# Layer norm of a cross-attention block: centering on ScalarE by the mean alone, rstd and gamma in one DVE operation in slot 3

## The chip, the cores and the metric
One core of one Trainium2 chip runs the whole program. The metric is device time in microseconds. The kernel before took 670.51 us (median of 3 runs, 669.41 to 670.66).

## The reference
A cross-attention block over 8 batches: 224 queries and 750 keys of width 512, 16 heads of 32.
```
q = queries @ Wq.T + bq;  k = keys @ Wk.T + bk;  v = values @ Wv.T + bv      (keys = values = ctx)
att = softmax(q k^T / sqrt(32));  out = concat_heads(att v) @ Wo.T + bo + queries
mean, var over the last axis (512)
out = (out - mean) / sqrt(var + 1e-5) * gamma + beta
```
The change touches only the last line. All inputs and outputs are float32.

## The kernel before, in words
Batches follow each other in one software pipeline. An iteration has 32 steps, in 4 slots of 8 (`UNIT`); one step does the scores of half a head (112 queries against 750 keys). A slot is one unit of 4 heads. In the steps, PE also does tasks for other batches: it transposes context and x, projects K, Q and V of the next batch, and in steps 18 and 21 (`O_STEPS`) projects the two halves (q = 0, 1) of the output of the batch before. The iterations are b = 0 to 7 and a last one, b = 8 (`B`), without scores, which only drains the pipeline: the tail. In b = 7 (`LAST`) there is no next batch, so from step 12 on PE has only scores, exponent scores, attention and the two output projections to do.

Each engine runs its own list in the order in which the code writes it; the waits are semaphores. The order of one step:
- PE: scores of the next step (`scores`, L523), for which the row maximum of two steps before must have been read from its bank (`RING` = 2); scores with keys on partitions for the exponential (L547); attention times v (`attend`, L563) and the column sums (`sum_keys`, L589); the task of the step (L512, L475).
- ScalarE: the high part of a saved task (L672, L674), the copy of the attention (L698), the maxima (`save_maxima`, L679, first step of a slot), the exponentials (`exp`, L690), the high part of the attention (`attn_high`, L704).
- DVE: the row maximum (`row_max`, L793), the save of a task (`save_task`, L755 to L770), reciprocals (L800), the attention scaling (L807) and its low part (L817), and at the end of a step the layer norm.
- GpSimd: the sums over keys of each head, three additions (L902, L907, L910) in steps 4, 5, 7 and the first step of the next slot, and its part of the layer norm.
- SP starts all DMAs, also in order: after the loads of the next inputs it stores half 0 (`store_half`, L383), fills the stacks of unit 0 of the next batch (`fill_stack`, L377 to L380, 16 DMAs), stores half 1, fills unit 1, and loads the residual (L368).

The layer norm of the batch before runs in this order. Step 19 or 22: DVE writes y = projection + residual from PSUM (L767) and its statistics (L770). Step 20 or 23: mean and variance (`mean_of`, L773). Same step, GpSimd: rstd (`rstd_of`, L920 and L922, a power of -0.5). Step 21 or 24: DVE's `center` (L777) subtracts the mean and multiplies by rstd. Steps 24 to 27: GpSimd multiplies by gamma (L926) and adds beta (L930), half 0 in steps 24 and 25, half 1 in steps 26 and 27. Then the half is stored. In the tail `center` comes in steps 22 and 25; GpSimd does gamma and beta of half 0, and DVE those of half 1 (L783, L785).

Of the kernel before, what the change touches and what calls it, by code (L numbers as in the profile page):

```python
# [7 lines left out]
ALU = mybir.AluOpType  # L8
ACT = mybir.ActivationFunctionType
# [6 lines left out]
def build(nc, x, ctx_tokens, Wq, bq, Wk, bk, Wv, bv, Wo, bo, gamma, beta, out):  # L16
# [68 lines left out]

    LN_STEP = 3 * UNIT
    SUM_STEPS = ((1, 4, 0), (1, 5, 1), (1, 7, 2), (2, 0, 3))
# [83 lines left out]
    with ExitStack() as stack:  # L171
# [71 lines left out]
        recip_ready, attn_scaled, attn_low_saved = sem("recip_ready"), sem("attn_scaled"), sem("attn_low_saved")  # L243
        last_sums_ready, last_scaled, last_ready = sem("last_sums_ready"), sem("last_scaled"), sem("last_ready")
        stats_ready, mean_ready, centered, bias_ready = sem("stats_ready"), sem("mean_ready"), sem("centered"), sem("bias_ready")
# [3 lines left out]
        pair_sums_ready, two_sums_ready, head_sums_ready = sem("pair_sums_ready"), sem("two_sums_ready"), sem("head_sums_ready")  # L249
        const_ready, resid_ready, var_eps_ready, rstd_ready = sem("const_ready"), sem("resid_ready"), sem("var_eps_ready"), sem("rstd_ready")  # L250
        y_scaled, y_ready = sem("y_scaled"), sem("y_ready")

# [104 lines left out]
        def _(sp):  # L357
# [55 lines left out]
            def iteration(b, parity):  # L413
# [13 lines left out]
                def store_half(q):  # L427
                    if q == 1 and isinstance(b, int) and b == B:
                        sp.wait_ge(last_ready, 1)
                    else:  # L430
                        sp.wait_ge(y_ready, 2 * (b - 1) + q + 1)
                    store(b - 1, q)
# [231 lines left out]
        def _(act):  # L664
# [28 lines left out]
            def copy_attn(u):  # L693
# [4 lines left out]
                nc.scalar.copy(attn_sums[:], source[:, :, 0:NQ]).then_inc(attn_copied, 1)  # L698

            def attn_high(u, g, task_n):  # L700
                act.wait_ge(attn_scaled, u + 1)
                if task_n is not None:
                    act.wait_ge(task_ready, task_n)
                nc.scalar.activation(attn_parts[:, 0, g, :], attn[:], ACT.Identity,  # L704
                                     bias=bias16["v"][:, g:g + 1]).then_inc(attn_high_saved, 1)
# [6 lines left out]
            def iteration(b, parity):  # L712
                tasks = iteration_tasks(b)
                before = tasks_before(b)
                for s in range(STEPS):
# [13 lines left out]
                    for u, g_u in due("high", b, s):  # L729

                        after_o = before + tasks[O_STEPS[1]][1] + 1 if g_u == 0 and has_output(b) else None
                        attn_high(u, g_u, after_o)
                    u = unit_before(b, g, 1)
                    if u is not None:
# [9 lines left out]
        def _(dve):  # L744
# [29 lines left out]

            def center(q, batch):
                dve.wait_ge(rstd_ready, 2 * batch + q + 1)
                nc.vector.tensor_scalar(y[0:QP, q], y[0:QP, q], mean_var[0:QP, q, 0:1], rstd[0:QP, q:q + 1],  # L777
                                        ALU.subtract, ALU.mult).then_inc(centered, 1)

            def gamma_beta(q, batch):  # L780

                dve.wait_ge(centered, 2 * batch + q + 1)
                nc.vector.tensor_tensor(y[0:QP, q], y[0:QP, q], rows["gamma"][0:QP], ALU.mult).then_inc(last_scaled, 1)  # L783
                dve.wait_ge(last_scaled, 1)
                nc.vector.tensor_tensor(y[0:QP, q], y[0:QP, q], rows["beta"][0:QP], ALU.add).then_inc(last_ready, 1)  # L785
# [48 lines left out]
            def iteration(b, parity):  # L834
                tasks = iteration_tasks(b)
                before = tasks_before(b)
                for s in range(STEPS):
# [24 lines left out]
                    for u, g_u in due("low", b, s):  # L862
                        attn_low(u, g_u)
                    last = isinstance(b, int) and b == B
                    wait_for_rstd = 4 if last else 3
                    if has_output(b) and s - wait_for_rstd in O_STEPS:
                        center(O_STEPS.index(s - wait_for_rstd), b - 1)
                        if last and s - wait_for_rstd == O_STEPS[1]:
                            dve.wait_ge(rows_loaded, 3 * DMA)
                            gamma_beta(1, b - 1)  # L870

# [6 lines left out]
        def _(pool):  # L878
# [44 lines left out]

            def times_gamma(q, batch):
                pool.wait_ge(centered, 2 * batch + q + 1)
                nc.gpsimd.tensor_tensor(y[0:QP, q], y[0:QP, q], rows["gamma"][0:QP], ALU.mult).then_inc(y_scaled, 1)  # L926

            def plus_beta(q, batch):
                pool.wait_ge(y_scaled, 2 * batch + q + 1)
                nc.gpsimd.tensor_tensor(y[0:QP, q], y[0:QP, q], rows["beta"][0:QP], ALU.add).then_inc(y_ready, 1)  # L930

            pool.wait_ge(rows_loaded, 3 * DMA)

            def iteration(b, parity):
                for s in range(STEPS):
# [5 lines left out]
                    if has_output(b):  # L941
                        for q in range(2):
                            if s == 9 + q:
                                add_bo(q, b - 1)
                            if s == O_STEPS[q] + 2:
                                rstd_of(q, b - 1)
                        last = isinstance(b, int) and b == B
                        for q in range(1 if last else 2):
                            at = O_STEPS[1] + 3 if last else LN_STEP + 2 * q
                            if s == at:  # L950
                                times_gamma(q, b - 1)
                            if s == at + 1:
                                plus_beta(q, b - 1)
# [24 lines left out]
```

## Time and profile before
The profiled execution took 670.35 us, with a span of 668.5 us from its first to its last instruction.

| | busy us | share of the span | instructions |
|---|---|---|---|
| PE (TensorE matmul) | 644.6 | 96% | 5441 |
| DVE (VectorE) | 480.5 | 72% | 680 |
| ACT (ScalarE) | 334.2 | 50% | 657 |
| POOL (GpSimd) | 456.0 | 68% | 458 |

The mean granted clock of PE is 0.988 of full speed. The chain of waits that ended last is 76% PE, 12% GpSimd, 5% DVE, 2% ScalarE. Matmuls are pipelined and their ends modelled, so a busy PE may hold small waits; a share is a mean over stages with different limits. The stretches, timelines and chains below give the time from the start of the span.

### The profile page before, as it was taken

To read this page: it belongs to the slowest core of one execution; us is meant where nothing else is said; L and a number is where in the kernel's file an instruction comes from. 1 tells how busy PE (TensorE), PEld (TensorE's weight loads), DVE (VectorE), ACT (ScalarE), POOL (GpSimd) and SP (SyncE) were. 2 spreads that over 40 slices of the span, in tenths; PEclk is the share of its full clock that TensorE was granted. 3 is DMA by queue.
4 is the path that set the end of the run, shared out by engine and by line. 5 is a ranking of instruction groups with operands and counts; after the bars stand their busy time and mean duration, and the time that the engine had idled before them with its cause. 6 is when DMAs were issued, how large, how long until landed. Compare 5 with 4: busy or idle time off the path is not lost.

```text
span 668.5 us, 15116 instructions
## 1 busy us (share of the span) xinstructions
PE 644.6 (96%) x5441; PEld 450.0 (67%) x5441; DVE 480.5 (72%) x680; ACT 334.2 (50%) x657; POOL 456.0 (68%) x458
## 2 busy tenths in 40 slices
PE   9999999999999999999999999999999999999893
PEld 8766676766777666776767667776677667665452
DVE  4676667778777686776767787776877777677775
ACT  4423645555455455554455554554555544555460
POOL 9302765876957688576858769576885868678942
PEclk9999999999999999999999999999999999999888
DMA  9383322231232223332133312322233201331010
GB/s 289 120 219 87 91 67 72 60 90 50 76 99 70 66 74 83 88 73 86 52 82 90 91 50 76 100 66 70 74 85 90 63 2 28 83 90 39 15 43 28
DMA packets 39562, 53.08 MB, mean 79 GB/s; under 512 B 13436, under 2 KB 25736, under 8 KB 39496
## 3 DMA queue, kind: packets, MB, share of 16 engines
q1 hardware_dynamic: 39496, 52.16, 29.2%
q8 instruction: 46, 0.75, 0.5%
q14 instruction: 20, 0.16, 0.1%
HBM read 24.52 MB, written 3.67 MB: 42 GB/s over the span
## 4 chain that ended last, share of the span: by engine, by line
PE 76%; POOL 12%; DVE 5%; issue 4%; ACT 2%; POOLq 0%; ACTq 0%; DVEq 0%
PE ps_task L512 34%; PE ps_scores L523 9%; PE ps_task L563 9%; PE ps_scoresT L547 8%; POOL pair_sums L902 6%; PE ps_task L475 6%; POOL head_sums L907 3%; POOL head_sums L910 2%; PE ps_scores L512 2%; PE ps_task L589 2%; ACT probsT L690 2%; DVE top L793 2%; PE ps_task L485 1%; DVE y L767 1%; DVE parts L755 1%
## 5 line engine op out<-in xcount | busy, mean ns | idle before, releaser
L793 DVE TENSOR_REDUCE top<-ps_scores 112x1 f32<-112x750 f32 x256 | 235.8, 928 | 115.6 <-PE ps_scores L523 114.5
L902 POOL TENSOR_TENSOR pair_sums<-probsT 125x672 f32<-125x672 f32 x122 | 199.1, 1632 | 163.5 <-ACT probsT L690 160.1
L690 ACT ACTIVATE probsT<-ps_scoresT 125x448 f32<-125x448 f32 x384 | 193.0, 545 | 156.8 <-PE ps_scoresT L547 153.9
L523 PE MATMUL ps_scores<-stacks 96*112 96x512 f16 (+1 forms) x512 | 126.6, 329 | 5.3 <-DVE top L793 4.1
L512 PE MATMUL ps_task<-wvT,ctxT 128*125 128x512 f16 x564 | 129.9, 380 | 0.8 <-DVE ctxT L757 0.7
L512 PE MATMUL ps_task<-ctxT,wkT 128*128 128x375 f16 x708 | 122.7, 323 | 0.1
L547 PE MATMUL ps_scoresT<-stacks 100*125 100x224 f16 x768 | 120.9, 264 | 2.0 <-ACT probsT L690 0.2
L547 PEld LDWEIGHTS ps_scoresT<-stacks 100*125 100x125 f16 x768 | 87.8, 138 | 35.0 <-ACT probsT L690 10.8
L512 PEld LDWEIGHTS ps_task<-wvT,ctxT 128*125 128x125 f16 x564 | 74.6, 136 | 40.0 <-DVE ctxT L757 0.9
L512 PEld LDWEIGHTS ps_task<-ctxT,wkT 128*128 128x128 f16 x708 | 68.7, 97 | 37.5 <-DVE v L760 0.5
L907 POOL TENSOR_TENSOR head_sums<-pair_sums 125x224 f32<-125x224 f32 x122 | 85.2, 698 | 10.4
L910 POOL TENSOR_TENSOR head_sums<-head_sums,pair_sums 125x224 f32<-125x224 f32 x122 | 80.9, 663 | 9.6
L563 PE MATMUL ps_task<-probsT,v 125*32 125x224 f32 x1488 | 81.3, 360 | 0.4 <-ACT attn_sums L698 0.4
L523 PEld LDWEIGHTS ps_scores<-stacks 96*112 96x112 f16 x512 | 59.2, 131 | 29.5 <-issue 18.3
L760 DVE COPY v<-ps_task 125x512 f32<-125x512 f32 x47 | 32.5, 692 | 43.1 <-PE ps_task L512 43.1
L563 PEld LDWEIGHTS ps_task<-probsT,v 125*32 125x32 f32 x1488 | 44.0, 110 | 27.9 <-issue 9.0
L672 ACT ACTIVATE parts<-ps_task,bk 128x375 f16<-128x375 f32 x59 | 33.8, 574 | 49.8 <-PE ps_task L512 49.8
L800 DVE RECIPROCAL recip<-attn_sums 128x112 f32<-128x112 f32 x64 | 53.5, 840 | 3.2 <-ACT attn_sums L698 3.2
L698 ACT COPY attn_sums<-ps_task 128x448 f32<-128x448 f32 x31 | 16.5, 533 | 71.7 <-PE ps_task L589 71.3
L475 PE MATMUL ps_task<-woT,attn_parts 128*112 128x512 f16 x192 | 44.3, 381 | 0.3
L512 PE MATMUL ps_task<-xT,wqT 128*128 128x224 f16 x360 | 39.4, 259 | 0.0
L755 DVE SCALAR_TENSOR_TENSOR parts<-ps_task,bk,parts 128x375 f16<-128x375 f32 x59 | 35.2, 597 | 1.0 <-ACT parts L672 1.0
(94 smaller groups left out, 592.0 us busy)
## 6 DMA issues: line engine op xcount, KB each, us to landing
stacks<-parts SPq DMA_DIRECT2D x256, 60.9 KB, 2.0
ctx_in<-in_ctx SPq DMA_DIRECT2D x16, 672.0 KB
stacks<-parts SPq DMA_DIRECT2D x128, 46.9 KB, 2.0
x_in<-in_x SPq DMA_DIRECT2D x8, 448.0 KB, 3.7
resid<-in_x SPq DMA_DIRECT2D x8, 448.0 KB, 3.8
out_y<-y SPq DMA_DIRECT2D x16, 224.0 KB, 2.3
stacks<-parts SPq DMA_DIRECT2D x128, 14.0 KB, 1.8
ctx_in<-in_ctx SPq DMA_DIRECT2D x16, 78.0 KB
```

Of the source, the lines that this page charges most:

```text
L475: last = nc.tensor.matmul(bank[0:QP, :], attn_parts[:, a, k, QP * q:QP * q + QP], wT["o"][:, c, k, :], start=(k == 0 and (a, c) == (0, 0)) ...
L512: last = nc.tensor.matmul(dst, lhsT, rhs, start=first, stop=(n_mm == 0))
L523: last = nc.tensor.matmul(ps_scores[0:QP, s % RING, keys], stacks[0:STACK_ROWS, g, h, NK + QP * q:NK + QP * q + QP], stacks[0:STACK_ROWS, ...
L547: last = nc.tensor.matmul(ps_scoresT[0:KP, piece % 2, NQ * i:NQ * i + NQ], stacks[:, g, h, KP * k:KP * k + KP], stacks[:, g, h, Qc], start ...
L563: last = nc.tensor.matmul(ps_attn[c:c + DK, 0:NQ], v[of_batch][0:KP, k, P * g + c:P * g + c + DK], probsT[0:KP, g % 2, h, k, :], start=(k ...
L690: nc.scalar.activation(probsT[0:KP, g % 2, h, 2 * j:2 * j + 2, :].rearrange("p k q -> p (k q)"), ps_scoresT[0:KP, piece % 2, 0:2 * NQ], AC ...
L755: nc.vector.scalar_tensor_tensor(dst, src, b16, high, ALU.add, ALU.subtract).then_inc(task_saved, 1)
L793: nc.vector.tensor_reduce(top[0:QP, g % 2, HG * q + h:HG * q + h + 1], ps_scores[0:QP, s % RING, 0:NK], AX.X, ALU.max).then_inc(top_ready, 1)
L800: nc.vector.reciprocal(recip[:, cols], attn_sums[:, 1, cols]).then_inc(recip_ready, 1)
L902: nc.gpsimd.tensor_tensor(pair_sums[0:KP], probsT[0:KP, g % 2, h, 0:3, :], probsT[0:KP, g % 2, h, 3:6, :], ALU.add).then_inc(pair_sums_rea ...
L907: nc.gpsimd.tensor_tensor(head_sums[0:KP, g % 2, h, :], pair_sums[0:KP, 0], pair_sums[0:KP, 1], ALU.add).then_inc(two_sums_ready, 1)
L910: nc.gpsimd.tensor_tensor(head_sums[0:KP, g % 2, h, :], head_sums[0:KP, g % 2, h, :], pair_sums[0:KP, 2], ALU.add).then_inc(head_sums_read ...
```

## The change
ScalarE gets `center`: y becomes mean - y, with the mean as bias column and a scale of -1, in steps 21 and 24, in the tail as well. GpSimd turns gamma's sign once, ahead of the first iteration, so that the product with it has the right sign. DVE's `times_gamma` multiplies y by rstd and by the turned gamma in one operation, in steps 26 and 28 (`GAMMA_STEPS`). GpSimd adds beta in steps 27 and 29. In the tail DVE adds beta to both halves, right behind each product, and GpSimd none. `store_half` waits in the tail for `last_ready` of its half.
```diff
@@ -83,7 +83,7 @@
             NU - 1: {"copy": 11, ("invert", 0): 12, ("invert", 1): 13, "scale": 14, "high": 15, "low": 16}}
     HIGH_STEP, LOW_STEP = STAGES["high"][1], STAGES["low"][1]
 
-    LN_STEP = 3 * UNIT
+    GAMMA_STEPS = (3 * UNIT + 2, 3 * UNIT + 4)
     SUM_STEPS = ((1, 4, 0), (1, 5, 1), (1, 7, 2), (2, 0, 3))
     assert UNIT + LOW_STEP < O_STEPS[0] and O_STEPS[1] < 2 * UNIT + HIGH_STEP
     STEP_OF = {t: s for s, t in {**OWN, **NEXT, **OUTPUT}.items()}
@@ -241,13 +241,14 @@
         top_ready, task_saved = sem("top_ready"), sem("task_saved")
         top_zero = sem("top_zero")
         recip_ready, attn_scaled, attn_low_saved = sem("recip_ready"), sem("attn_scaled"), sem("attn_low_saved")
-        last_sums_ready, last_scaled, last_ready = sem("last_sums_ready"), sem("last_scaled"), sem("last_ready")
+        last_sums_ready, last_ready = sem("last_sums_ready"), sem("last_ready")
         stats_ready, mean_ready, centered, bias_ready = sem("stats_ready"), sem("mean_ready"), sem("centered"), sem("bias_ready")
 
         ones_ready, ident_zero, ident_ready = sem("ones_ready"), sem("ident_zero"), sem("ident_ready")
         pick_zero, pick_ready = sem("pick_zero"), sem("pick_ready")
         pair_sums_ready, two_sums_ready, head_sums_ready = sem("pair_sums_ready"), sem("two_sums_ready"), sem("head_sums_ready")
         const_ready, resid_ready, var_eps_ready, rstd_ready = sem("const_ready"), sem("resid_ready"), sem("var_eps_ready"), sem("rstd_ready")
+        gamma_turned = sem("gamma_turned")
         y_scaled, y_ready = sem("y_scaled"), sem("y_ready")
 
         def need(eng, s, value):
@@ -425,8 +426,8 @@
                     load_ctx(b + 2, half)
 
                 def store_half(q):
-                    if q == 1 and isinstance(b, int) and b == B:
-                        sp.wait_ge(last_ready, 1)
+                    if isinstance(b, int) and b == B:
+                        sp.wait_ge(last_ready, q + 1)
                     else:
                         sp.wait_ge(y_ready, 2 * (b - 1) + q + 1)
                     store(b - 1, q)
@@ -697,6 +698,12 @@
                 source = (ps_attn if not is_last(u) else ps_scores[:, 0]).rearrange("p (a q) -> p a q", a=2)
                 nc.scalar.copy(attn_sums[:], source[:, :, 0:NQ]).then_inc(attn_copied, 1)
 
+            def center(q, batch):
+
+                act.wait_ge(mean_ready, 2 * batch + q + 1)
+                nc.scalar.activation(y[0:QP, q], y[0:QP, q], ACT.Identity, bias=mean_var[0:QP, q, 0:1],
+                                     scale=-1.0).then_inc(centered, 1)
+
             def attn_high(u, g, task_n):
                 act.wait_ge(attn_scaled, u + 1)
                 if task_n is not None:
@@ -730,6 +737,8 @@
 
                         after_o = before + tasks[O_STEPS[1]][1] + 1 if g_u == 0 and has_output(b) else None
                         attn_high(u, g_u, after_o)
+                    if has_output(b) and s - 3 in O_STEPS:
+                        center(O_STEPS.index(s - 3), b - 1)
                     u = unit_before(b, g, 1)
                     if u is not None:
                         for piece in pieces_of(b, s, True):
@@ -772,16 +781,15 @@
             def mean_of(q):
                 nc.vector.bn_aggr(mean_var[0:QP, q], stats[0:QP, q]).then_inc(mean_ready, 1)
 
-            def center(q, batch):
+            def times_gamma(q, batch):
+
+                dve.wait_ge(centered, 2 * batch + q + 1)
                 dve.wait_ge(rstd_ready, 2 * batch + q + 1)
-                nc.vector.tensor_scalar(y[0:QP, q], y[0:QP, q], mean_var[0:QP, q, 0:1], rstd[0:QP, q:q + 1],
-                                        ALU.subtract, ALU.mult).then_inc(centered, 1)
-
-            def gamma_beta(q, batch):
-
-                dve.wait_ge(centered, 2 * batch + q + 1)
-                nc.vector.tensor_tensor(y[0:QP, q], y[0:QP, q], rows["gamma"][0:QP], ALU.mult).then_inc(last_scaled, 1)
-                dve.wait_ge(last_scaled, 1)
+                nc.vector.scalar_tensor_tensor(y[0:QP, q], y[0:QP, q], rstd[0:QP, q:q + 1], rows["gamma"][0:QP],
+                                               ALU.mult, ALU.mult).then_inc(y_scaled, 1)
+
+            def last_beta(q, batch):
+                dve.wait_ge(y_scaled, 2 * batch + q + 1)
                 nc.vector.tensor_tensor(y[0:QP, q], y[0:QP, q], rows["beta"][0:QP], ALU.add).then_inc(last_ready, 1)
 
             def row_max(s, T, unit):
@@ -861,13 +869,11 @@
                         scale_attn(u)
                     for u, g_u in due("low", b, s):
                         attn_low(u, g_u)
-                    last = isinstance(b, int) and b == B
-                    wait_for_rstd = 4 if last else 3
-                    if has_output(b) and s - wait_for_rstd in O_STEPS:
-                        center(O_STEPS.index(s - wait_for_rstd), b - 1)
-                        if last and s - wait_for_rstd == O_STEPS[1]:
-                            dve.wait_ge(rows_loaded, 3 * DMA)
-                            gamma_beta(1, b - 1)
+                    if has_output(b) and s in GAMMA_STEPS:
+                        dve.wait_ge(gamma_turned, 1)
+                        times_gamma(GAMMA_STEPS.index(s), b - 1)
+                        if isinstance(b, int) and b == B:
+                            last_beta(GAMMA_STEPS.index(s), b - 1)
 
             batches(dve, iteration)
 
@@ -921,15 +927,12 @@
                 pool.wait_ge(var_eps_ready, 2 * batch + q + 1)
                 nc.gpsimd.tensor_tensor(rstd[0:QP, q:q + 1], var_eps[0:QP, q:q + 1], minus_half[0:QP], ALU.pow).then_inc(rstd_ready, 1)
 
-            def times_gamma(q, batch):
-                pool.wait_ge(centered, 2 * batch + q + 1)
-                nc.gpsimd.tensor_tensor(y[0:QP, q], y[0:QP, q], rows["gamma"][0:QP], ALU.mult).then_inc(y_scaled, 1)
-
             def plus_beta(q, batch):
                 pool.wait_ge(y_scaled, 2 * batch + q + 1)
                 nc.gpsimd.tensor_tensor(y[0:QP, q], y[0:QP, q], rows["beta"][0:QP], ALU.add).then_inc(y_ready, 1)
 
             pool.wait_ge(rows_loaded, 3 * DMA)
+            nc.gpsimd.tensor_scalar(rows["gamma"][0:QP], rows["gamma"][0:QP], -1.0, None, ALU.mult).then_inc(gamma_turned, 1)
 
             def iteration(b, parity):
                 for s in range(STEPS):
@@ -944,12 +947,8 @@
                                 add_bo(q, b - 1)
                             if s == O_STEPS[q] + 2:
                                 rstd_of(q, b - 1)
-                        last = isinstance(b, int) and b == B
-                        for q in range(1 if last else 2):
-                            at = O_STEPS[1] + 3 if last else LN_STEP + 2 * q
-                            if s == at:
-                                times_gamma(q, b - 1)
-                            if s == at + 1:
+                        for q in range(2):
+                            if s == GAMMA_STEPS[q] + 1 and not (isinstance(b, int) and b == B):
                                 plus_beta(q, b - 1)
 
             batches(pool, iteration)
```

## Rows read from the trace of the kernel before

**Rows 1.** Busy time in stretches of 1 us: stretch, length, busy of each engine, PEclk, DMA.
```profile
609.00:610.00 1.00, 0.38 (x3) 0.26 (x3) 1.00 (x2) 0.26 (x1) 1.00 (x1) 1.00 0.51 125
...
628.00:629.00 1.00, 0.05 (x1) 0.09 (x2) 1.00 (x2) 0.00 (x0) 0.92 (x2) 0.81 0.00 0
629.00:630.00 1.00, 1.00 (x5) 0.79 (x6) 1.00 (x2) 0.00 (x0) 1.00 (x2) 0.50 0.07 16
...
638.00:639.00 1.00, 1.00 (x10) 0.30 (x7) 0.99 (x2) 0.55 (x2) 1.00 (x1) 0.57 0.77 211
```

**Rows 2.** Chain that ended last, 624 to 642 us: start, us, what.
```profile
626.13 1.82 DVE y L777
627.95 0.86 DVE top L793
...
628.95 0.84 PE ps_scores L523 x2
...
638.81 0.57 PE ps_scoresT L547 x4
```

**Rows 3.** Timeline of PE, last batch: start, us, what, idle before and its releaser.
```profile
614.97 0.53 PE L523 MATMUL ps_scores<-stacks 96*112 96x512 f16 x2
...
616.33 0.53 PE L523 MATMUL ps_scores<-stacks 96*112 96x512 f16 x2
...
625.89 0.59 PE L563 MATMUL ps_task<-probsT,v 125*32 125x224 f32 x8
...
640.21 0.41 PE L532 MATMUL ps_scoresT<-ident,top 112*128 112x112 f32 x2
```

**Rows 4.** Timeline of GpSimd, last batch.
```profile
626.06 1.60 POOL L902 TENSOR_TENSOR pair_sums<-probsT 125x672 f32<-125x672 f32 x1
```

**Rows 5.** Groups of instructions: what, times (x), busy us, mean ns of one, idle before.
```profile
L704 ACT ACTIVATE attn_parts<-attn,bv 128x224 f16<-128x224 f32 x32 | 15.4, 482 | 2.6 <-DVE attn L807 2.6
...
L783 DVE TENSOR_TENSOR y<-y,gamma_row 112x512 f32<-112x512 f32 x1 | 1.6, 1564 | 0.1
...
L785 DVE TENSOR_TENSOR y<-y,beta_row 112x512 f32<-112x512 f32 x1 | 0.7, 692 | 0.0
```

**Rows 6.** Lines L777 and L817 alone: duration ns min/median/max.
```profile
L777 DVE TENSOR_SCALAR y<-y,mean_var,rstd x16: 531/1243/1825, 160.6 to 662.0; 112x512 f32<-112x512 f32 x16
...
L817 DVE SCALAR_TENSOR_TENSOR attn_parts<-attn,bv,attn_parts x32: 420/443/1773, 88.4 to 656.1; 128x224 f16<-128x224 f32 x32
```

**Rows 7.** Chain that ended last, the tail.
```profile
659.02 0.18 DVE mean_var L773
...
660.50 0.45 DVE y L777
...
661.97 1.49 DVE y L777
...
665.15 0.69 DVE y L785
```

**Rows 8.** Loop: the stretch 240 to 260; timelines of DVE, PE, GpSimd and SP's queue.
```profile
240.00:260.00 20.00, 20.00 (x179) 14.55 (x177) 15.40 (x24) 10.45 (x21) 17.83 (x19) 1.00 0.20 57
...
257.18 0.44 DVE L755 SCALAR_TENSOR_TENSOR parts<-ps_task,bq,parts 128x224 f16<-128x224 f32 x1
...
259.14 2.08 PE L512 MATMUL ps_task<-ctxT,wkT 128*128 128x375 f16 x12
...
256.31 1.61 POOL L902 TENSOR_TENSOR pair_sums<-probsT 125x672 f32<-125x672 f32 x1
...
252.49 0.51 SPq L379 DMA_DIRECT2D stacks<-parts  x1
```

**Rows 9.** Timeline of DVE, last batch.
```profile
624.09 0.91 DVE L793 TENSOR_REDUCE top<-ps_scores 112x1 f32<-112x750 f32 x1
...
628.72 0.84 DVE L800 RECIPROCAL recip<-attn_sums 128x112 f32<-128x112 f32 x1
...
638.15 5.03 DVE L812 TENSOR_REDUCE head_sums<-probsT 125x224 f32<-125x1344 f32 x2
```

## The prediction

> **What bounds the kernel now.** I read four views in this order: the busy time in stretches, the timelines of the last batch, the chain of waits that ended last, and the groups of instructions with their durations.
>
> The stretches first. In the body of the run TensorE (PE) has no free moment: 20.00 of 20.00 us between 240 and 260 us, at full clock [rows 8]. An engine other than PE can therefore bring nothing there by being quicker; it can only do harm by being late. The reader is to see in the one-microsecond stretches that this ends in the last batch: PE is all but idle in 628 to 629 (0.05 busy), its granted clock drops there (mean 0.81), stands at 0.50 (the 1.2 GHz level) in 629 to 630 and is back in 638 to 639 (0.57) [rows 1]. The chain of waits names what held PE: the centering of half 1 on DVE (L777) starts at 626.13 after GpSimd's rstd, takes 1.82, then the row maximum behind it takes 0.86, then PE's scores start at 628.95 [rows 2]. PE's last matmuls before that end at 626.48 [rows 3], so the hole is 2.47 us. PE then does four steps (one pair of score matmuls each) from 628.95 to 638.81, 2.46 each [rows 2], where the same step took 1.36 at full clock (614.97 to 616.33) [rows 3].
>
> The tail is a second place that ends the run: after PE's last matmul the chain is DVE and GpSimd alone, with the centering of half 1 at 661.97 (1.49), gamma on DVE (1.57) and beta (0.69), ending at 665.84; 2.66 of the span of 668.5 follow, the last store [rows 7].
>
> **Part 1: the slots before the last one (steps 21 and 24 of each batch).** Two L777 go from DVE and two ScalarE instructions of 112x512 come. No row shows such a one. The nearest is L704, SBUF to SBUF with a bias column, 0.482 for 224 columns [rows 5]: below, 0.48; above, 1.10 if it all scaled with the columns. I take 0.7, nearer the low end, because time doesn't scale with the columns in the rows of DVE either (0.69 for 512 [rows 5], 0.44 for 224 [rows 6]). In the last batch it stands behind the two exponentials of step 21 and behind the copy of the maxima in step 24, while PE runs the output projection or has two steps without exponentials; both ends fit in these holes, so it costs nothing. If that cover were gone it would delay the exponentials behind it by its own 0.7. It needs the mean alone, so ScalarE does not wait for GpSimd's rstd. Gain in the loop: none, since PE was never idle for these (above).
>
> **Part 2: slot 3 (steps 26 and 28).** DVE gets two operations with two SBUF inputs of 512 columns. The nearest row is the addition of beta, L785, 0.69 [rows 5]; below 0.53 (the shortest L777 [rows 6]); above, what another engine adds: the same shape took 1.56 (L783) while GpSimd was in an operation of its own [rows 5], and the longest L777 is 1.82 against 0.53 at least [rows 6]. In the last batch L777 from 626.13 ended at 627.95, 0.29 after GpSimd's operation that began at 626.06 and took 1.60 [rows 2, 4]: DVE waited until it had ended. So one operation costs 0.69, and up to 1.3 more if it meets the long pair sum of GpSimd.
>
> The SBUF page of the Trainium skill (SBUF — State Buffer, the part with the port rules) says that a DVE instruction with two SBUF inputs and a GpSimd instruction that reads SBUF lock each other out, whichever comes second waiting for all of the first. That speaks against putting the new operation at step 28, beside GpSimd's sums. The 0.29 and the 1.56 above agree. By the rule step 28 pays the wait in every batch and the sum is the one below; without it the loop term would be zero and the last batch 0.9 better.
>
> In the loop, step 28: the operation comes at 256.35, GpSimd is by then in the pair sum of the second head (at 256.31 before [rows 8], at some 255.7 now, with two operations fewer ahead of it), so I give it 1.5. The row maximum and the save of the Q task move back: that save stands at 257.18 before, ending at 257.6, and PE takes the bank at 259.14 [rows 8]. 1.5 later it ends at 259.1, so PE waits 0 to 0.1: 6 full batches, 0 to 0.6 in sum, I take +0.2. Step 26 meets an idle GpSimd (gamma is no longer there) and a DVE with a pause; nothing waits.
>
> **Part 3: GpSimd.** It loses 15 multiplications, keeps 14 of the betas, now behind the sums of step 29, and gains one multiplication by -1 at the start, when it has nothing else to do before the first head sums. The first store is issued when beta of half 0 is done, some 1.7 later than before in the loop. SP has the 16 stack transfers of the next batch behind it, but those wait for the Q save of about the same moment (issued from 252.49 [rows 8]). The scores that need the first head come behind PE's task of 259.14 [rows 8]: over 6.5 us for four transfers issued 0.6 apart. The second store stood behind these transfers anyway. Cost 0; without this cover it would be the delay itself, 0.3 a batch.
>
> **Part 4: the last batch.** Walk DVE from the end of the row maximum at 625.0 [rows 9]. Up to the last row maximum stand 6 of them (0.87 apart, back to back), 2 reciprocals (0.84 [rows 9], 0.8 apart), two new operations at 0.69, and two attention operations of 0.44 (the median of L817 [rows 6]): 5.2 + 1.6 + 1.4 + 0.9 = 9.1, so 634.1 if nothing blocks. Four of these read two SBUF tensors while GpSimd is busy almost without a gap; each may wait up to 1.3, in all 5.2: 639.3. Walking both engines side by side, GpSimd ends its operation 0.3 to 0.5 into two of them: I take 0.9 in all, 635.0. PE alone could be there at 626.48 + 4 x 1.36 + 1.4 = 633.3. It needs that last row maximum for the transposes at 640.21 [rows 3]. So these begin at 635.1: **-5.1**, made of 2.5 of stall and 4.4 of clock less 1.8 of new, shorter waits of PE for row maxima. Ends: -6.9 (PE alone) and -0.9 (blocked every time). GpSimd has two multiplications less before its next head sums; DVE's own two head sums (5.03 from 638.15 [rows 9]) shift by 3.1, end near 640.1, and the matmuls that take them come at about 641.5, so they hold nothing. Everything behind moves by the same amount.
>
> Will the clock stay? The new waits are 0.4 to 0.8 each, 1.8 in some 8 us. At 609 to 610 PE was busy 0.38 of 1.00, with smaller holes in the three microseconds before, and the clock stayed at 1.00 [rows 1]. So I take it that it does.
>
> **Part 5: the tail.** The mean of half 0 ends at 659.20 [rows 7]; ScalarE centers it by 659.9 behind DVE's own work. The mean of half 1 no longer stands behind L777 (0.45 in the chain from 660.50 [rows 7]) and ends at 660.70. DVE: gamma for half 0 to 661.4, beta to 662.1. Half 1 is centered by 661.5 and its rstd ready by 661.65 (GpSimd's steps from 661.05, 0.35 to 0.4 earlier), both before DVE is free. Then gamma to 662.8, beta to 663.5. GpSimd is quiet now, so nothing is blocked. 665.84 - 663.5 = **-2.3**, from -1.5 (one more wait of 0.8) to -2.5. The first store is issued 1.4 ahead of the last as before (1.3), so the 2.66 stay.
>
> **Sum.** -5.1 - 2.3 + 0.2 = -7.2. The profiled execution took 670.35 (span 668.5 and 1.85 around it): 663.15. The median of the runs shown, 670.51, is 0.16 above it. I say 663.2.
>
> **Rivals.**
> (a) The clock falls all the same, because the new waits together thin PE out as much as the one hole did. For it: the hole and the waits lie in the same stretch. Against it: rows 1 at 609. Only the stall is then won: -2.5 - 2.3 + 0.2, 665.8.
> (b) DVE is blocked at each of its four operations in the last batch: -0.9 there, 667.3. Against: in the rows the blocked ones are a minority (L817 has a median of 0.44 against a longest of 1.77 [rows 6]).
> (c) Slower: the operation at step 28 isn't let in between GpSimd's operations until the head's three sums are over (1.6 + 0.7 + 0.7 from 255.7), so it ends at 259.3 and the Q save at 260.5. PE stands 1.4 in each of 6 batches and, with the other blocked ones in the last, where -0.9 is left, the sum is +8.4 - 0.9 - 2.3 = +5.2: 675.6. It decides from a stall of 0.6 a batch in that case. Against it: no blocked row is longer than one pair sum plus its own time.
> (d) PE alone sets the last batch (-6.9): 661.2.
>
> **Chances.** Forecast 0.68, (a) 0.14, (b) 0.06, (c) 0.05, (d) 0.07. The likeliest one's own range is 662.2 to 664.6. The range for 8 in 10 goes from (d) past (a): 661.0 to 666.5. Faster by over 0.2% (about what a measurement of this kernel can tell from no change) 0.91, within 0.2% 0.04, slower 0.05.
>
> **What would show it.** In the new profile: no hole of PE above 1 us between 624 and 636 and a clock of 1.00 there; three or four waits of the scores for DVE's row maximum of 0.3 to 0.8; the two new DVE operations at 0.7 in the tail, and above 1.2 at step 28 in the loop; the centering on ScalarE near 0.7 with nobody waiting for it; from PE's last matmul to the last beta 5.3 to 5.5 instead of 7.7; loop batches as long as before within 0.1. I am wrong if the clock falls between 624 and 640, if PE shows waits in the loop at step 30, or if ScalarE's centering holds DVE in the tail.

## The result, and the profile after

| | before | after |
|---|---|---|
| median of 6 runs, us | 670.70 (669.41 to 676.68) | 663.82 (663.25 to 665.25) |
| profiled execution, us (span) | 670.35 (668.5) | 663.89 (662.0) |
| mean granted clock of PE | 0.988 | 0.997 |
| busy us: PE, DVE, ScalarE, GpSimd | 644.6, 480.5, 334.2, 456.0 | 639.9, 478.8, 344.6, 441.2 |

The ratio of the two is 0.9889, 95% interval 0.9864 to 0.9914. Beside later experiments the same kernel gave 0.9884 (0.9863 to 0.9905) and 0.9872 (0.9855 to 0.9889). The forecast was 663.2 for the median and 663.15 for the profiled execution.

The lines that answer to the row maximum and the hole behind it [rows 1 to 3], from the timeline of PE in the last batch; in brackets the idle time before and who ended it:
```profile
625.38 0.58 PE L564 MATMUL ps_task<-probsT,v 125*32 125x224 f32 x8
625.89 0.53 PE L524 MATMUL ps_scores<-stacks 96*112 96x512 f16 x2
...
629.39 0.50 PE L524 MATMUL ps_scores<-stacks 96*112 96x512 f16 x2 [0.71 <-DVE top L801]
...
634.91 0.41 PE L533 MATMUL ps_scoresT<-ident,top 112*128 112x112 f32 x2 [1.10 <-DVE top L801]
```
The scores that stood 2.47 us now follow without a gap (625.89), two waits are left behind them (0.71 and 1.10), and the transposes of the row maxima ("the turned maxima" from here on) come at 634.91 instead of 640.21. The stretches of 1 us (length, busy of PE, PEld, DVE, ScalarE, GpSimd, then PEclk, DMA) show PE thin at times and the clock at 1.00 all the same:
```profile
628.00:629.00 1.00, 0.68 (x10) 0.16 (x8) 1.00 (x2) 0.98 (x2) 1.00 (x2) 1.00 0.00 0
629.00:630.00 1.00, 0.61 (x5) 0.55 (x6) 1.00 (x3) 0.42 (x1) 1.00 (x1) 1.00 0.00 0
...
634.00:635.00 1.00, 0.09 (x1) 0.09 (x2) 1.00 (x3) 0.41 (x1) 0.86 (x2) 1.00 0.00 0
```
DVE in the same batch (answers to [rows 9]):
```profile
627.55 0.85 DVE L788 SCALAR_TENSOR_TENSOR y<-y,rstd,gamma_row 112x512 f32<-112x512 f32 x1
...
630.32 2.48 DVE L788 SCALAR_TENSOR_TENSOR y<-y,rstd,gamma_row 112x512 f32<-112x512 f32 x1
...
634.78 4.97 DVE L820 TENSOR_REDUCE head_sums<-probsT 125x224 f32<-125x1344 f32 x2
```
and GpSimd beside the second product (answers to [rows 4]):
```profile
628.88 1.81 POOL L932 TENSOR_TENSOR y<-y,beta_row 112x512 f32<-112x512 f32 x1
630.64 1.61 POOL L908 TENSOR_TENSOR pair_sums<-probsT 125x672 f32<-125x672 f32 x1
632.39 0.93 POOL L913 TENSOR_TENSOR head_sums<-pair_sums 125x224 f32<-125x224 f32 x1
```
The product that came at 630.32 ended at 632.80, 0.55 behind the end of the pair sum. I read this as a wait for the beta (to 630.69) and then for the pair sum (to 632.25) too.

The groups of the new instructions (times, busy us, mean ns; idle before) and line L788 alone (ns min/median/max), which answer to [rows 5, 6]:
```profile
L788 DVE SCALAR_TENSOR_TENSOR y<-y,rstd,gamma_row 112x512 f32<-112x512 f32 x16 | 18.4, 1148 | 0.5 <-POOL rstd L928 0.5
...
L704 ACT ACTIVATE y<-y,mean_var 112x512 f32<-112x512 f32 x16 | 11.8, 737 | 4.5 <-DVE mean_var L782 4.3
```
```profile
L788 DVE SCALAR_TENSOR_TENSOR y<-y,rstd,gamma_row x16: 740/800/2482, 171.8 to 657.8; 112x512 f32<-112x512 f32 x16
```
The tail begins with DVE's first y, here from the chain that ended last, before and after:
```profile
657.56 0.70 DVE y L767
```
```profile
652.67 0.70 DVE y L776
```
and from the timeline of all engines after the change (answers to [rows 7]):
```profile
654.38 0.19 POOL L926 TENSOR_TENSOR var_eps<-mean_var,eps 112x1 f32<-112x1 f32 x1 [5.48 <-DVE mean_var L782]
654.65 0.55 POOL L928 TENSOR_TENSOR rstd<-var_eps,minus_half 112x1 f32<-112x1 f32 x1
...
655.64 0.18 DVE L782 BATCH_NORM_AGGREGATE mean_var<-stats 112x2 f32<-112x6 f32 x1
655.76 0.75 DVE L788 SCALAR_TENSOR_TENSOR y<-y,rstd,gamma_row 112x512 f32<-112x512 f32 x1
655.86 0.72 ACT L704 ACTIVATE y<-y,mean_var 112x512 f32<-112x512 f32 x1 [0.80 <-DVE mean_var L782]
655.90 0.66 POOL L926 TENSOR_TENSOR var_eps<-mean_var,eps 112x1 f32<-112x1 f32 x1 [0.70 <-DVE mean_var L782]
656.54 0.69 DVE L793 TENSOR_TENSOR y<-y,beta_row 112x512 f32<-112x512 f32 x1
656.63 1.01 POOL L928 TENSOR_TENSOR rstd<-var_eps,minus_half 112x1 f32<-112x1 f32 x1
...
657.78 0.75 DVE L788 SCALAR_TENSOR_TENSOR y<-y,rstd,gamma_row 112x512 f32<-112x512 f32 x1 [0.55 <-POOL rstd L928]
658.57 0.69 DVE L793 TENSOR_TENSOR y<-y,beta_row 112x512 f32<-112x512 f32 x1
```
From the first y of the tail to the end of the last beta it takes 6.59 instead of 8.28. The row to look at is GpSimd's: its two one-column operations take 0.19 and 0.55 for half 0, and 0.66 and 1.01 for half 1, beside DVE's product and beta.

The loop at step 28 (answers to [rows 8]), DVE, then PE, then SP's queue:
```profile
255.49 1.51 DVE L788 SCALAR_TENSOR_TENSOR y<-y,rstd,gamma_row 112x512 f32<-112x512 f32 x1
...
257.77 0.44 DVE L764 SCALAR_TENSOR_TENSOR parts<-ps_task,bq,parts 128x224 f16<-128x224 f32 x1
...
258.27 2.08 PE L513 MATMUL ps_task<-ctxT,wkT 128*128 128x375 f16 x12
...
251.87 0.56 SPq L380 DMA_DIRECT2D stacks<-parts  x1
```
The save of Q ends at 258.21 and PE goes on at 258.27 without an idle time in its row. The first stack transfer is issued at 251.87; PE's row has moved by 0.87, so the transfer is 0.25 later than before. All six products of step 28 in the loop took 1.51.

**Where the time went**, by the same instruction in both profiled executions: at the first wait of PE for a parts save (44.16, now 43.57) the new one is already 0.59 ahead, in a stretch that the change doesn't touch; at the fourth wait of the last batch (609.65, 609.14) 0.51, so seven batches cost 0.08; at the turned maxima 5.30, so 4.79 come from the last batch; at the first y of the tail 4.89, so 0.41 is lost on the way; at the last beta 6.58 (1.69 from the tail); at the end 6.5. The first 0.59 is not the change's: e1 and e4 below, whose first batches are those of the kernel before, have that wait at 43.54 and 43.53. The 0.08 is no finer than the executions are: ahead of the scores at 264 PE waits 1.04 before and 1.46 after, and between 0.88 and 1.74 in the other profiles.

### The profile page after: what moved, and what is told of

It is laid out like the page before. It is cut to its first block, busy times and chain, and to the rows that moved or that the text cites. A ratio compares the mean times of both kernels' runs of the same rounds, so it can differ in the third digit from the quotient of the medians.

```text
span 662.0 us, 15140 instructions
## 1 busy us (share of the span) xinstructions
PE 639.9 (97%) x5441; PEld 446.9 (68%) x5441; DVE 478.8 (72%) x680; ACT 344.6 (52%) x673; POOL 441.2 (67%) x443
## 4 chain that ended last, share of the span: by engine, by line
PE 75%; POOL 9%; DVE 9%; issue 4%; ACT 2%; POOLq 0%; DVEq 0%; ACTq 0%
PE ps_task L513 35%; PE ps_scores L524 9%; PE ps_task L564 8%; PE ps_scoresT L548 8%; PE ps_task L476 6%; POOL pair_sums L908 5%; DVE top L801 3%; PE ps_scores L513 2%; POOL head_sums L913 2%; POOL head_sums L916 2%; PE ps_task L590 2%; ACT probsT L691 2%; PE ps_task L486 1%; DVE recip L808 1%; DVE y L776 1%
## 5 line engine op out<-in xcount | busy, mean ns | idle before, releaser
L524 PE MATMUL ps_scores<-stacks 96*112 96x512 f16 (+1 forms) x512 | 125.2, 326 | 3.9 <-DVE top L801 2.3
L548 PE MATMUL ps_scoresT<-stacks 100*125 100x224 f16 x768 | 119.4, 261 | 2.1 <-ACT probsT L691 0.2
L548 PEld LDWEIGHTS ps_scoresT<-stacks 100*125 100x125 f16 x768 | 86.3, 136 | 34.6 <-ACT probsT L691 11.1
L913 POOL TENSOR_TENSOR head_sums<-pair_sums 125x224 f32<-125x224 f32 x122 | 86.9, 712 | 10.4
L916 POOL TENSOR_TENSOR head_sums<-head_sums,pair_sums 125x224 f32<-125x224 f32 x122 | 82.7, 678 | 9.6
L564 PE MATMUL ps_task<-probsT,v 125*32 125x224 f32 x1488 | 79.7, 355 | 0.0
```

The lines of the kernel that those rows point to most:

```text
L524: last = nc.tensor.matmul(ps_scores[0:QP, s % RING, keys], stacks[0:STACK_ROWS, g, h, NK + QP * q:NK + QP * q + QP], stacks[0:STACK_ROWS, ...
L548: last = nc.tensor.matmul(ps_scoresT[0:KP, piece % 2, NQ * i:NQ * i + NQ], stacks[:, g, h, KP * k:KP * k + KP], stacks[:, g, h, Qc], start ...
L564: last = nc.tensor.matmul(ps_attn[c:c + DK, 0:NQ], v[of_batch][0:KP, k, P * g + c:P * g + c + DK], probsT[0:KP, g % 2, h, k, :], start=(k ...
L913: nc.gpsimd.tensor_tensor(head_sums[0:KP, g % 2, h, :], pair_sums[0:KP, 0], pair_sums[0:KP, 1], ALU.add).then_inc(two_sums_ready, 1)
L916: nc.gpsimd.tensor_tensor(head_sums[0:KP, g % 2, h, :], head_sums[0:KP, g % 2, h, :], pair_sums[0:KP, 2], ALU.add).then_inc(head_sums_read ...
```

## Experiments

The first four ran beside each other and beside the kernel before, whose median there was 671.58; the others beside 671.98 and 671.93. One span is common to all of them and shows the last batch alone: from PE's fourth wait for a row maximum (609.65 before) to the turned maxima (640.21). It is 30.56 before and 25.77 after. The fourth wait, before and after:
```profile
609.65 0.53 PE L523 MATMUL ps_scores<-stacks 96*112 96x512 f16 x2 [0.62 <-DVE top L793]
```
```profile
609.14 0.53 PE L524 MATMUL ps_scores<-stacks 96*112 96x512 f16 x2 [0.62 <-DVE top L801]
```

**e1: only the place of DVE's centering.** Edit to the kernel before:
```diff
-                    wait_for_rstd = 4 if last else 3
+                    wait_for_rstd = 4 if last else 5 if isinstance(b, int) and b == LAST else 3
```


> The kernel before, with one change: in iteration 7 DVE's centering (mean and rstd, as before) comes in steps 23 and 26 instead of 21 and 24. GpSimd keeps gamma and beta, ScalarE gets nothing. My theory: what the change won in the last batch is the place of DVE's operation that waits for rstd; where it is doesn't matter before, so this alone removes the 2.5 us hole of PE at 626 and keeps the clock at 1.00. Some waits of 0.5 to 1.5 for row maxima remain: 3.5 to 4.6 us faster than the kernel before (about 666.5). Rival: it is the division of the work (GpSimd freed of gamma, ScalarE taking the centering) that brings it; then the hole only moves a step and the time stays within 1.5 us of before.


Measured: 666.00 (665.00 to 667.59), ratio 0.9938 (0.9914 to 0.9962): faster by 4.2 by the ratio, by 5.6 by the medians. The last batch takes 25.14, even less than after the change. Its centerings, with the mean and rstd as before, no longer meet a wait:
```profile
624.01 0.73 DVE L777 TENSOR_SCALAR y<-y,mean_var,rstd 112x512 f32<-112x512 f32 x1
...
628.66 0.71 DVE L777 TENSOR_SCALAR y<-y,mean_var,rstd 112x512 f32<-112x512 f32 x1
```
So what the last batch gained is a matter of place. Neither ScalarE's share nor GpSimd's lighter load was needed for it.

**e2: the whole change, with the product back in steps 21 and 24.**
```diff
-                    if has_output(b) and s in GAMMA_STEPS:
+                    at = GAMMA_STEPS if isinstance(b, int) and b == B else (O_STEPS[0] + 3, O_STEPS[1] + 3)
+                    if has_output(b) and s in at:
```


> The changed kernel, with DVE's product with rstd and gamma back in steps 21 and 24 (before the tail; the tail is that of the changed kernel). Betas stay in steps 27 and 29. My theory: DVE again waits for rstd and then for GpSimd's pair sum ahead of a row maximum, so the PE hole of 2 to 2.8 us comes back near 626, the clock falls to 0.50 for some 10 us, and all of the last batch's gain is lost: 667.5 to 669.5, about 2 us better than the kernel before (its tail). Rival (division of work): stays at 664 to 665.


Measured: 670.34 (666.89 to 672.55), ratio 0.9993 (0.9964 to 1.0022): slower than my bracket of 667.5 to 669.5; a gain can't be told from zero. The hole is back, behind rstd and the pair sum:
```profile
628.32 1.98 DVE L788 SCALAR_TENSOR_TENSOR y<-y,rstd,gamma_row 112x512 f32<-112x512 f32 x1 [1.35 <-POOL rstd L929]
```
```profile
631.30 0.84 PE L524 MATMUL ps_scores<-stacks 96*112 96x512 f16 x2 [2.85 <-DVE top L801]
```
The last batch takes 32.25. For the last batch, e1 and e2 together show from both sides that the place of the operation decides. The 672.13 of this profiled execution are not all of that hole, though. Its clock also fell early in the run, behind PE's wait of 0.72 for a saved task ahead of 83.5: mean 0.51 from 84 to 86 and 0.64 from 86 to 88, where one V projection took 4.49 instead of 2.80. No other profile shows a low clock there, with the same wait.

**e3: the hole filled with idle work, to part the stall from the clock.**
```diff
+                    if isinstance(b, int) and b == LAST and s == 27:
+                        pe.wait_ge(task_saved, tasks_before(LAST) + len(tasks_of(LAST)))
+                        for _ in range(10):
+                            nc.tensor.matmul(ps_task[:, 0, 0:P], ident[:], ident[:], start=True, stop=True)
```


> The kernel before, with 10 additional matmuls of 128x128 f32 on a free bank in step 27 of iteration 7, ahead of the scores that wait for DVE. They do nothing for the result; they fill the hole of 2.5 us. My theory: the hole costs twice, its length and the clock behind it. Then the scores still start at 629 (span position), the clock stays at 1.00, and the four steps behind take 1.4 to 1.9 instead of 2.46 each, DVE's row maxima being next: 3.5 to 4.6 faster than before, about 666.5. Rival: the clock is not the cause of the slow steps but what DVE and GpSimd do there; then nothing is won (670 to 671).


Measured: 667.45 (666.38 to 669.90), ratio 0.9963 (0.9940 to 0.9986). PE's timeline:
```profile
626.95 2.50 PE L621 MATMUL ps_task<-ident 128*128 128x128 f32 x20
629.50 0.50 PE L523 MATMUL ps_scores<-stacks 96*112 96x512 f16 x2
...
630.96 0.53 PE L523 MATMUL ps_scores<-stacks 96*112 96x512 f16 x2
...
632.59 0.50 PE L523 MATMUL ps_scores<-stacks 96*112 96x512 f16 x2 [0.21 <-DVE top L797]
```
The scores still wait out the same 2.5 us, but the steps behind take 1.33 to 1.63 instead of 2.46. The last batch takes 26.75: 3.8 less, all of it clock, since the scores behind the hole start no earlier. The change, which removes the hole as well, has 25.77. That is 1.0 less again and not 2.5, because DVE's row maxima are next to hold PE (the waits of 0.71 and 1.10).

**e4: only the new tail.** The loop is that of the kernel before; in the tail:
```diff
-                nc.vector.tensor_tensor(y[0:QP, q], y[0:QP, q], rows["gamma"][0:QP], ALU.mult).then_inc(last_scaled, 1)
-                dve.wait_ge(last_scaled, 1)
+                dve.wait_ge(rstd_ready, 2 * batch + q + 1)
+                nc.vector.scalar_tensor_tensor(y[0:QP, q], y[0:QP, q], rstd[0:QP, q:q + 1], rows["gamma"][0:QP],
+                                               ALU.mult, ALU.mult).then_inc(last_scaled, 1)
+                dve.wait_ge(last_scaled, q + 1)
...
+                if isinstance(b, int) and b == B:
+                    nc.gpsimd.tensor_scalar(rows["gamma"][0:QP], rows["gamma"][0:QP], -1.0, None, ALU.mult).then_inc(gamma_turned, 1)
```


> The kernel before in all iterations with scores, and the tail of the changed one: ScalarE centers, DVE multiplies by rstd and gamma and adds beta for both halves; gamma's sign is turned at the start of the tail. From the trace of the changed kernel, whose tail from the first y to the last beta takes 6.6 us instead of 8.3: 1.7 faster than before, about 669.0. If the parts of the change are independent, e1's or e3's gain plus this one must give the whole. The forecast's -2.3 for the tail would give 668.4.


Measured: 669.73 (667.01 to 671.33): 1.85 under its median beside it, ratio 0.9989 (0.9962 to 1.0017), so the runs alone don't prove it. The trace does: from the first y to the last beta it takes 6.60 instead of 8.28. Every profile with the new tail has 6.59 to 6.62, every one with the old 8.27 or 8.28. Its profile has the same stall of 2.47, but the low clock behind it was over after four microseconds, not ten, and its last batch took 27.87:
```profile
628.00:630.00 2.00, 1.24 (x10) 0.86 (x14) 2.00 (x3) 0.51 (x2) 1.92 (x3) 0.83 0.04 8
630.00:632.00 2.00, 2.00 (x14) 1.06 (x6) 2.00 (x5) 0.52 (x3) 1.92 (x3) 0.50 0.00 0
632.00:634.00 2.00, 2.00 (x20) 0.97 (x22) 1.33 (x3) 1.58 (x4) 1.92 (x2) 0.82 0.37 115
```
The same hole is thus paid with different lengths of low clock from one execution to the next: against e3's 26.75, with no low clock, it cost 3.8 in the profile before and 1.1 here.

The next three ran beside the changed kernel itself:

> The changed kernel, unaltered, as the measure for the three beside it: 663.3 to 665.3 as in its first runs, and a span near 662.


Measured: 663.66 (663.13 to 664.79), span of the profiled execution 662.4.

**e5: who slows rstd in the tail.** Edit to the changed kernel:
```diff
-                        if isinstance(b, int) and b == B:
-                            last_beta(GAMMA_STEPS.index(s), b - 1)
+                        if isinstance(b, int) and b == B and s == GAMMA_STEPS[1]:
+                            for q in range(2):
+                                last_beta(q, b - 1)
```


> The changed kernel; in the tail DVE adds beta to half 0 after the product of half 1 instead of before it. My theory of the 0.6 that the tail fell short of the forecast (-1.7 for -2.3): GpSimd's two small operations for rstd of half 1 wait while DVE is in an operation with two SBUF inputs (0.66 and 1.01 instead of 0.19 and 0.55), and DVE's product waits for them. Then the second one is back at 0.55 here, since no beta stands beside it, the first stays at 0.66 (the product of half 0), and the product of half 1 starts about 0.5 earlier, 4.6 after the first y instead of 5.1. The end stays where it was within 0.2, since beta of half 0 now stands behind it. Rival: the small operations are slow for another reason (a first use, a late wake-up); then the second still takes about 1.0.


Measured: 663.92 (663.61 to 664.23) against 663.66. The timeline of its tail:
```profile
655.66 0.66 POOL L927 TENSOR_TENSOR var_eps<-mean_var,eps 112x1 f32<-112x1 f32 x1 [0.71 <-DVE mean_var L782]
656.39 0.55 POOL L929 TENSOR_TENSOR rstd<-var_eps,minus_half 112x1 f32<-112x1 f32 x1
657.09 0.75 DVE L788 SCALAR_TENSOR_TENSOR y<-y,rstd,gamma_row 112x512 f32<-112x512 f32 x1 [0.82 <-POOL rstd L929]
```
Without a beta beside it rstd is back at 0.55, the one beside the product stays at 0.66, and the product of half 1 starts 4.67 after the first y (652.42) instead of 5.11. The theory holds for the second operation. That the first stays at 0.66 fits it, but nothing was moved away from that one.

**e6: the residual loaded earlier; e7: the last product in step 30.** Both edit iteration 7 of the changed kernel:
```diff
+                if isinstance(b, int) and b == LAST:
+                    load_resid(b)
                 if has_output(b):
                     store_half(1)
...
-                if has_output(b) and has_step(b, 0):
+                if has_output(b) and has_step(b, 0) and not (isinstance(b, int) and b == LAST):
...
+                        if isinstance(batch, int) and batch == LAST:
+                            dve.wait_ge(stored, 2 * DMA * LAST)
```
```diff
-                    if has_output(b) and s in GAMMA_STEPS:
+                    at = (26, 30) if isinstance(b, int) and b == LAST else GAMMA_STEPS
+                    if has_output(b) and s in at:
```


> The changed kernel; in iteration 7 SP loads the residual of the last batch ahead of the second store instead of behind it, and DVE waits for the stores ahead of the tail's first y. My theory of the 0.4 lost between 640 and 658: the beta of half 1 comes later, the store and the load behind it too, and GpSimd's two additions of bo (2.65) fall on DVE's low part of the attention (1.54 instead of 0.45) ahead of PE's output projection. Here they come before 643, that low part takes 0.45, PE's waits ahead of the projection (0.31 and 0.71) shrink, and the span is 0.3 to 0.9 shorter. Rival: the matmuls ahead set it and the span stays.

> The changed kernel; in iteration 7 the product of half 1 comes in step 30, behind the last row maximum, instead of in step 28 (where it took 2.48, through two operations of GpSimd). PE's wait of 1.10 ahead of the turned maxima should go, and PE reach them about 1 us earlier. My theory: DVE's own two head sums of 5 us stand behind the product in both and are on the chain of the last 25 us, so hardly anything reaches the end: -0.4 to 0. Rival: PE sets that stretch and the end comes 1.0 earlier. The residual comes later still, which may cost up to 0.5.


Measured: 664.04 (662.82 to 664.75) and 663.11 (662.64 to 664.43), against 663.66 (663.13 to 664.79) of the changed kernel. Neither can be told from it. e6's additions of bo come at 640.18 and the low part of the attention takes 0.45; but the second profile of the changed kernel has them at 647.40, too late to meet it, with 0.45 as well. So most of this loss comes and goes: from the turned maxima to the first y it took 17.35 before, 17.76 in the first profile, 17.44 in the second and 17.48 in e6. In e7 PE reaches the turned maxima without the wait of 1.10, and gives 0.4 to 0.7 back behind it (18.15 to the first y). DVE's own head sums hold the rest, as expected: from their start to the first y it takes 17.57 in the second profile of the changed kernel and 17.62 in e7.

**Both edits, and the thin stretch filled.** e8 has the edits of e6 and e7; e9 is the changed kernel, e10 is e8's, with
```diff
+    FILL = {15: 1, 16: 1, 17: 1, 18: 3}
...
+                    if isinstance(b, int) and b == LAST and s in FILL:
+                        pe.wait_ge(task_saved, before + saved_by(b, 10))
+                        for _ in range(FILL[s]):
+                            nc.tensor.matmul(ps_task[:, 0, 0:P], ident[:], ident[:], start=True, stop=True)
```


> The changed kernel, unaltered, as the measure for the three beside it. In its second profile the clock fell at 608, behind four waits of PE for row maxima (0.24, 0.21, 0.22, 0.62), and in the first it did not; runs should again lie in two groups, near 663.3 with a mean clock of 0.995 to 0.997 and near 665 with 0.993.

> The changed kernel with both edits of iteration 7 tried before: the residual loaded ahead of the second store (e6) and the product of half 1 in step 30 (e7). Each alone took 0.3 or less. Theory: PE's wait ahead of the turned maxima goes, and GpSimd's additions of bo come before DVE needs the lock: 0.3 to 0.8 below the changed kernel beside it. Rival: the chain through DVE's head sums holds both, and the two are the same within 0.3.

> The changed kernel with 6 additional matmuls (128x128 f32, on a free bank, of no use for the result) ahead of the scores of steps 15 to 18 in iteration 7, where PE waits four times for row maxima. Theory: they take the place of these waits (0.2 each), so PE is not thin there and the clock never falls at 608: no run with a mean clock of 0.993, the slow group of the changed kernel is gone and the median is 0 to 0.7 lower, the runs closer together. Rival: the clock falls by something else than PE's idle share; then the two groups stay, and the extra matmuls cost up to 0.5.

> e8's kernel with the same 6 matmuls. If both theories hold: 662.3 to 663.0 in all runs, the fastest of the four. If only that of the clock holds: as e9.


Measured: 663.18 (the changed kernel), 663.57, 663.97 and 663.54. None is better: e8's profile has the shortest span (660.8 against 661.3 beside it), its runs lie between 662.65 and 664.46. Its last batch takes 24.59 against 25.76 in the profile beside it, and 0.73 of that 1.17 is given back before the first y. The matmuls of e9 did fill the stretch (busy 2.00 of 2.00 from 608 to 610, 1.38 without), but cannot be shown to keep the clock: without them 8 of 31 runs had a mean clock of 0.993 or 0.994, with them 1 of 10. Three of the eight have a profile (the second of the changed kernel, e6 and e7), and in all three the clock fell between 608 and 612; the one of e10 has none, and after e2 it could have fallen near 84 as well. How busy PE is ahead of the fall does not tell the executions apart. The third profile of the changed kernel, then e6, both with 1.56 of 2.00 in the stretch before:
```profile
608.00:610.00 2.00, 1.38 (x16) 0.77 (x14) 2.00 (x3) 0.85 (x2) 1.92 (x2) 1.00 0.26 62
```
```profile
608.00:610.00 2.00, 1.38 (x7) 0.92 (x6) 1.88 (x3) 0.48 (x1) 1.92 (x2) 0.70 0.25 62
```
So this stretch is where the clock fell when it fell, and whether filling it prevents that stays open. None of these versions is shown to be faster than the changed kernel.

## Why the prediction was right

**What bounds.** Right, and shown from both sides by e1 and e2: the wait for rstd and the pair sum ahead of a row maximum. That the hole cost more by its clock (3.8) than by its length (2.47) in the profiled execution is shown by e3.

**Part 1 (ScalarE).** 0.7 forecast, 0.737 mean (0.72 in the median), and no engine was idle for it, in the tail either.

**Part 2 (the product in the loop).** 1.5 forecast at step 28, 1.51 measured; PE idle 0.0, all batches before the last 0.08 against +0.2. The operation alone takes 0.74, not 0.69: the beta's row was 0.05 short. The port rule of the Trainium skill (SBUF — State Buffer, the section "Who interferes with whom") has the second of the two engines wait, whichever it is. The traces agree in both directions: DVE's 1.51 beside a pair sum, GpSimd's 1.01 for 0.55 beside a beta (e5).

**Part 4 (last batch).** -5.1 forecast, -4.8 measured. The sum was near by two errors against each other. For blocked operations of DVE I had allowed 0.9 in all. They cost 1.85: 0.11 in the first product (0.85 for 0.74), nothing in the attention's two operations (0.38, 0.43), and 1.74 in the second product, 2.48 through two operations of GpSimd, where I had capped every block at one. Against that, DVE's list itself was shorter than the walk. From 624.49 (the 625.0 of the walk, less 0.51) to the end of the last row maximum (634.85) are 10.36, so 8.5 without the blocks, where the walk had 9.1. The new waits of PE were two, 0.71 and 1.10, where I had expected three or four of 0.3 to 0.8; their sum is 1.8 as forecast, but the second is above the 1 us that I had named as the bound.

**The clock.** It stayed, as forecast, but my ground was weak: I took from one stretch of one execution (609 to 610) that small waits leave it alone. The second profile of the changed kernel shows the clock falling just there:
```profile
606.00:608.00 2.00, 1.33 (x8) 0.57 (x6) 2.00 (x4) 1.84 (x3) 1.83 (x2) 1.00 0.28 70
608.00:610.00 2.00, 1.61 (x10) 1.18 (x14) 2.00 (x3) 0.51 (x2) 1.84 (x3) 0.65 0.21 50
610.00:612.00 2.00, 2.00 (x12) 0.71 (x5) 0.06 (x1) 0.47 (x2) 1.86 (x2) 0.50 0.04 8
```
Its last batch takes 27.27, 1.5 more than the first profile's. So waits of 0.2 to 0.6 can be enough for it. They are the same before the change, and behind the new waits (624 to 640) the clock is 1.00 in every profile with the product in steps 26 and 28. Rival (a) therefore did not come, but the argument that I had against it is wrong.

**What the sum did not have.** The 0.4 between the maxima and the tail: the later beta of half 1 moves the second store, the load of the residual behind it, and GpSimd's additions of bo onto DVE's low part of the attention (1.54 for 0.45, PE 0.31 idle). I had followed the store only for the loop. e6 and the second profile do not have that low part of 1.54, and there only 0.1 is lost (17.44 and 17.48 for 17.35).

**Part 5 (tail).** -2.3 forecast, -1.7 measured. The step that was mis-sized is "GpSimd is quiet now, so nothing is blocked": DVE's own operations block GpSimd's rstd, 0.47 and 0.46, and DVE then waits for it (0.55). e5 shows it. The bound of -1.5 had been meant for such a wait. From PE's last matmul (653.28) to the last beta it is 5.98, not 5.3 to 5.5.

**Luck.** 0.59 of the span's 6.5 is the start of the program, so the change itself brought 5.9 where 7.2 was forecast. And the term of 4.4 for the clock was read from one execution, with some ten microseconds of low clock. From e4's last batch (27.87, four microseconds) the change to 25.77 would have been 2.1, an estimate. The median of the kernel before moved too: beside the later experiments (671.98, 671.93) the changed kernel is 8.3 and 8.8 faster, in the first runs 6.9. The forecast of the time is therefore closer than the knowledge of its terms.

**Rivals.** (b) and (d) did not come: the measured -4.8 lies between them. (d)'s own terms give 661.35, not 661.2. (c) did not come: no product of the loop took longer than 1.51.

## What to carry to other kernels

Look for the place where an engine in order waits for a slow helper ahead of what the bound engine needs next, and move the waiting operation behind it; the arithmetic may stay as it is (e1 brought most of the gain). Price a hole of PE with the low clock behind it, and from several executions, since the length of that low clock changes. Where two engines exclude each other, ask for the block in both directions and for more than one operation in a row.

## What the runs showed of the hardware

The kernel before, in 47 executions, lies between 665.5 and 672.4 of span, and largely goes with the clock: 4 executions at a mean clock of 0.993 have 665.5 to 666.0, 10 at 0.984 have 668.9 to 670.1; but 9 at 0.988 lie from 668.0 to 671.7. The change took away not only time but most of this spread (661.1 to 663.4 in 14 executions, 0.993 to 0.997).

The granted clock is not decided by the program alone. Behind the same hole of 2.47 it stayed low for some ten microseconds in one execution and for four in another. In two stretches where PE is equally thin in the profiles of these kernels (608 to 610, and near 84) it fell in some executions and not in others.

A DVE operation with two SBUF inputs can wait for two GpSimd operations in a row (2.48 us), when the second is issued as the first ends (630.64 beside 630.69). It ended 0.55 behind the second.
